# Gate rows and modulation columns of the first turns issued later, and the input of the state scan issued five places sooner in every turn

## What is computed

```
mod = (silu(L0_c) @ L0_wmod).reshape(2, 6, 1, -1)
sa, ca, ga, sb, cb, gb = mod[:, 0], mod[:, 1], ...
ga = (2 * (ga >= 0) - 1) * maximum(abs(ga), 0.25)      # gb the same
h = layernorm(x) * (1 + ca) + sa
x = x + ga * gated_linear_attention(h)                 # chunks of 64, 4 heads
h = layernorm(x) * (1 + cb) + sb
x = x + gb * small_per_channel_mlp(h)
# layer 1, with its own mod from L1_c, L1_wmod
x = x + ga * selective_state_scan(layernorm(x) * (1 + ca) + sa)
x = x + gb * expert_choice_moe(layernorm(x) * (1 + cb) + sb)   # 8 experts
```

## Time and profile before

| what | value |
|---|---|
| median of 3 runs | 1844.66 us |
| the profiled execution | 1847.26 us, span 1845.5 us |
| PE busy | 1696.9 us (92%) |
| DVE busy | 1475.3 us (80%) |
| ACT busy | 1362.8 us (74%) |
| POOL busy | 1369.7 us (74%) |
| first u on DVE | 142.89 us |
| DVE's u of the turns 2 to 15 | every 80.49 us |
| last POOL product of the scan | ends at 1420.8 us |

### The profile page before, as it was taken

How to read it: one execution, slowest core, us unless ns; L and a number is a source line. 1 busy time by engine, 2 the same in 40 slices (tenths; PEclk the granted TensorE clock), 3 DMA queues, 4 the chain that set the end, 5 groups by cost and what they waited for, 6 DMA issues and landing times.

```text
span 1845.5 us, 33565 instructions
## 1 busy us (share of the span) xinstructions
PE 1696.9 (92%) x12092; PEld 1454.0 (79%) x12092; DVE 1475.3 (80%) x3084; ACT 1362.8 (74%) x2673; POOL 1369.7 (74%) x644
## 2 busy tenths in 40 slices
PE   6788999999999999999999999998776999999998
PEld 5566787888878888787888878787565888899997
DVE  3557898898989889888988988888898678766663
ACT  3458879888887988888788888877643756666664
POOL 0008899998989989898998989899999333444443
PEclk8989999999999999999999999999998999999999
DMA  4011121122122112212211221212213444555552
GB/s 195 1 34 65 59 75 66 58 75 82 48 86 75 70 53 75 82 56 82 72 70 61 67 82 61 82 61 80 69 52 99 130 105 108 137 138 137 135 135 29
DMA packets 69461, 149.76 MB, mean 81 GB/s; under 512 B 5936, under 2 KB 43312, under 8 KB 68912
## 3 DMA queue, kind: packets, MB, share of 16 engines
q1 hardware_dynamic: 57008, 130.84, 20.6%
q0 software_dynamic: 12288, 16.79, 5.2%
HBM read 121.91 MB, written 17.30 MB: 75 GB/s over the span
## 4 chain that ended last, share of the span: by engine, by line
PE 73%; DVE 7%; issue 7%; POOL 6%; ACT 6%; DMA 0%; POOLq 0%; DVEq 0%; ACTq 0%
PE po L1820 10%; PE ph L1820 9%; PE pD L1118 9%; PE pY L1135 8%; PE pA L722 6%; DVE room L1167 3%; POOL room L1176 3%; PE pB L914 3%; PE pB L924 3%; POOL room L1186 3%; PE pB L1214 3%; PE pB L945 2%; PE pA L621 2%; PE pA L656 2%; PE pB L930 2%
## 5 line engine op out<-in xcount | busy, mean ns | idle before, releaser
L1186 POOL TENSOR_TENSOR room<-room 128x1024 f32<-128x1024 f32 x256 | 607.2, 2372 | 168.7 <-DVE room L1101 144.0
L1167 DVE TENSOR_TENSOR_SCAN room<-pD,last,room 128x256 f32<-128x256 f32 x1024 | 690.1, 732 | 43.0 <-PE pD L1118 31.7
L1176 POOL TENSOR_TENSOR room<-room 128x1024 f32<-128x1024 f32 x256 | 607.3, 2373 | 62.1 <-PE pY L1135 61.5
L1148 ACT ACTIVATE room<-room,fixed,kkT 128x512 f32<-128x512 f32 x512 | 406.6, 807 | 54.7 <-PE pD L1118 52.7
L1118 PE MATMUL pD<-fixed,room 128*128 128x128 f32 x2048 | 316.6, 278 | 60.3 <-DVE room L1167 49.1
L1135 PE MATMUL pY<-fixed,room 128*128 128x128 f32 x2048 | 315.5, 277 | 11.4 <-POOL room L1176 11.4
L1118 PEld LDWEIGHTS pD<-fixed,room 128*128 128x128 f32 x2048 | 240.0, 143 | 93.2 <-issue 44.1
L1135 PEld LDWEIGHTS pY<-fixed,room 128*128 128x128 f32 x2048 | 246.6, 144 | 61.6 <-POOL room L1176 24.1
L341 POOL DMA_INDIRECT xg<-xn_rows,W x64 | 67.5, 1054 | 196.5 <-DVE W L335 181.0
L1779 ACT ACTIVATE h<-ph 128x512 f32<-128x512 f32 x128 | 76.7, 599 | 137.8 <-PE ph L1820 107.1
L1820 PE MATMUL po<-w_up,h_up 128*128 128x256 f32 x512 | 149.6, 292 | 3.2 <-DVE h_rest L1687 2.6
(11 more groups left out here) (313 smaller groups left out, 3507.4 us busy)
## 6 DMA issues: line engine op xcount, KB each, us to landing
room<-kq_rows SPq DMA_DIRECT2D x128, 512.0 KB, 3.9
w_in<-w_d SPq DMA_DIRECT2D x32, 1024.0 KB
room<-ndS SPq DMA_DIRECT2D x16, 512.0 KB, 3.2
xt<-x_in SPq DMA_DIRECT2D x16, 256.0 KB, 2.9
y_out<-xo SPq DMA_DIRECT2D x16, 256.0 KB, 2.1
xn_rows<-xnC SPq DMA_DIRECT2D x16, 256.0 KB, 2.2
W<-weights SPq DMA_DIRECT2D x1, 1808.0 KB, 9.5
W<-weights SPq DMA_DIRECT2D x1, 1697.5 KB, 17.1
```

The lines of the kernel that those rows point to most:

```text
L1148: act.activation(decT[:, m % 2, t, :], turn2(ndT, it, NT * DI, t * DI, DI), ACT.Identity, bias=ones_s[:, 0:1], scale=turn2(kkT, it, NT * D ...
L1167: dve.tensor_tensor_scan(run, pD[h][:, k2 * TB:(k2 + 1) * TB], run, last[:, bass.ds(later(it) * (DS * DT) + m * DT + k, 1)], ALU.mult, ALU ...
L1176: pool.tensor_tensor(sq[:, m % 2], st[:, m % 4], kqb[:, m % SLOTS, 1, :].unsqueeze(1).broadcast_to([P, DT, TB]), ALU.mult).then_inc(sem("r ...
L1186: pool.tensor_tensor(st[:, m % 4], turn2(u, it, DT * TB).rearrange("p (k t) -> p k t", k=DT), kqb[:, m % SLOTS, 0, :].unsqueeze(1).broadca ...
```

## The change

Two things change place. First, in the prologue: layer 0's columns for the second norm move from step 10 to 22 (their copy from 12 to 24), layer 1's columns from steps 18 and 24 of turn -1 to its steps 60 and 63, the first three gate rows from 12, 18 and 69 to 34, 64 and 73, and the first fold from 34 to 44. The fold is split: `wo_g` needs only the first gate and stays with it, `wout_g` and the bias wait for the second gate and move to step 69. Second, u moves from 69 to 64 in all turns.

```
-    sig1=56, den=57, nd=60, ut=61, u=69, ...
+    sig1=56, den=57, nd=60, ut=61, u=64, ...
...
-                    pe.wait_ge(sem("folded"), 1 + B)
+                    pe.wait_ge(sem("folded"), 2)
...
-        MODS_AT, ROWS_AT, OUT_AT = (18, 24), (12, 18, STEPS + 5, STEPS + 20), STEPS + 30
-        FOLDS_AT = (34, STEPS + 5, STEPS + 6, STEPS + 7, STEPS + 8)
+        MODS_AT, ROWS_AT, OUT_AT = (60, 63), (34, STEPS, STEPS + 9, STEPS + 20), STEPS + 30
+        FOLDS_AT = (44, STEPS + 5, STEPS + 6, STEPS + 7, STEPS + 8)
...
-            if n == 10:                     # early_pe: columns of layer 0, second norm
+            if n == 22:
...
-            if n == 12:                     # early_dve: their copy
+            if n == 24:
...
+                dve.wait_ge(sem("grows"), 3)
+                for b in range(B):
+                    for c in range(DC):
+                        i = dve.tensor_tensor(wo_g[:, b, c, :], wo_n[:, c, :], gmul[:, 0, b * D:(b + 1) * D], ALU.mult)
+                i.then_inc(sem("folded"), 1)
+            if n == FOLDS_AT[1]:
                 dve.wait_ge(sem("grows"), 6)
```

More of the change, by code:

```diff
@@ L65 @@
     xs0=45, xs1=46, inz0=50, sz0=46, dkq_mm=50, dkq=52, inz1=51, sz1=52, kturn=53, kk=53, dt0=53, dt1=55, sig0=54,
-    sig1=56, den=57, nd=60, ut=61, u=69, yz0=19, yz1=19, yt0=21, yT0=20, yt1=22, yT1=22, out=25, x_scan=28, ln_d=40,
+    sig1=56, den=57, nd=60, ut=61, u=64, yz0=19, yz1=19, yt0=21, yT0=20, yt1=22, yT1=22, out=25, x_scan=28, ln_d=40,
     rows_d=42, turn_d=74, mod_d=75, score=79, scores=81, dec=11, sum=22, open0=21, open1=24, dec_t=6, saved=21,
@@ L1375, in early_dve @@
                 dve.wait_ge(sem("folded"), 1)
+                dve.wait_ge(sem("grows"), 3)
[4 more added lines that the diff above has]
+            if n == FOLDS_AT[1]:
                 dve.wait_ge(sem("grows"), 6)
                 for b in range(B):
-                    ga0, gb0 = (gmul[:, g, b * D:(b + 1) * D] for g in range(2))
-                    for c in range(DC):
-                        dve.tensor_tensor(wo_g[:, b, c, :], wo_n[:, c, :], ga0, ALU.mult)
+                    gb0 = gmul[:, 1, b * D:(b + 1) * D]
                     dve.tensor_tensor(wout_g[:, b, :], fo("wout2"), gb0, ALU.mult)
-                    dve.tensor_tensor(bg[:, b, :], fo("bout"), gb0, ALU.mult).then_inc(sem("folded"), 1)
+                    i = dve.tensor_tensor(bg[:, b, :], fo("bout"), gb0, ALU.mult)
+                i.then_inc(sem("folded"), 1)
             for part, at in enumerate(FOLDS_AT[1:4]):
                 if n == at:
-                    dve.wait_ge(sem("folded"), 1 + B + 2 * part)
+                    dve.wait_ge(sem("folded"), 3 + 2 * part)
                     dve.tensor_copy(bpart[:, :, :], bg[:, :, :]).then_inc(sem("folded"), 1)
-                    dve.wait_ge(sem("folded"), 1 + B + 2 * part + 1)
+                    dve.wait_ge(sem("folded"), 3 + 2 * part + 1)
                     row = slice(32 * part, 32 * part + 1)
```

## The result

| kernel | median | lowest to highest | runs | ratio to before, 95% interval |
|---|---|---|---|---|
| before | 1844.36 us | 1842.62 to 1845.01 | 6 | |
| after | 1853.03 us | 1851.28 to 1853.65 | 6 | 1.0047 [1.0036, 1.0058] |

The change makes the kernel 8.7 us slower. The profiled execution of after took 1851.96 us, with a span of 1850.1 and a mean granted clock of 0.975.

What follows compares the result with a forecast made beforehand. PE was taken to pace inner turns, POOL the last ones. Prologue -1.0, first boundary +0.3 and inner turns +11.3 make +10.6 us, 1844.66 to 1855.3 us; forecast range 1851 to 1860.5, 8-in-10 range 1845.5 to 1861.

Steps and rivals of the forecast that it cites:

- Part 1: Turn ends: u ahead of the statistics delays `og` and PE's restart by 0.87 us, 13 times, 11.3 us lost.
- The cushion: DVE's wait for ACT ahead of `og`, 0.31 us, taken off u's length of 1.18 us.
- the first boundary: First turn end with u: DVE waited 0.96 us ahead of `og`, so only 0.3 us is lost.
- Part 2: Prologue up to L630: products moved off the chain gain 6.7 us, 8.1 if z is fast, 5.2 if slow.
- Part 3: Prologue work put back on the chain in three groups, costing 1.8, 2.0 and 1.9 us.
- (a): First gate row ahead of the scores, with DVE operations and fold behind it: costs 1.8 us.
- (b): Two column groups and second gate row around the sum of squares: cost 2.0 us, bounds 0.8 and 4.
- (c): Third gate row moved onto the chain just before L890: costs 1.9 us, bounds 0.4 and 3.2.
- A: Rival: the turns absorb u's delay, only the prologue's effect is left, 1844.0 us; chance 0.11.
- D: Rival: prologue as forecast, but only half of the loop's delay carries, 1849.7 us; chance 0.10.
- B: Rival: POOL gains from the sooner u, 0.28 us in each of thirteen turns, 1840.1 us; chance 0.06.
- C: Rival: all 1.18 us count in 14 turns and the prologue loses its upper bound, 1865.8 us; chance 0.07.

Runs made afterwards that it cites:

- experiment 1: Kernel after, with its changed prologue, but u back at its old step 69: 1843.22 us against 1844.46, ratio 0.9993.
- experiment 2: Kernel before, with its old prologue, and only u moved, to step 64: 1853.84 us, ratio 1.0052.
- experiment 4: Kernel before with u at step 67, behind `og` and ahead of the sum: 1862.3 us, ratio 1.0091.
- experiment 5: Kernel before with u at step 68, which gave DVE the same instruction order as step 67: 1861.96 us, ratio 1.009.
- Experiment 7: Kernel after with u at step 69 and the third gate row back at its old step: 1841.76 us, ratio 0.9981.
- experiment 9: Kernel after with u at 69, third gate row at its old step and layer 1's columns behind the sum of turn 0: 1838.76 us, ratio 0.9965.
- experiment 3: Kernel before, u kept at step 69, its two products computed a second time into scratch at step 64: 1856.8 us, ratio 1.0058.
- experiment 6: Kernel before with u behind the sum and its statistics, directly ahead of the scan pair PE waits for: 1865.17 us, ratio 1.0109.

## Why the prediction was right

**Direction, mechanism and sum were right.** Forecast 1855.3, measured 1853.0. The prologue's part is small (forecast 1.0 gained, experiment 1: 1.2, not told from none) and u is the whole loss (forecast 11.6, experiment 2: 9.4). In the profiles, after loses 2.67 + 6.64 = 9.3 us against before from the sum of turn 1 to that of turn 15.

**Part 1, size per turn.** Forecast 0.87 us, measured 0.71. The cushion was 0.45 us and not the 0.31 of the wait's row. Before, `og` started 0.32 us behind the listed end of the scan pair ahead of it (776.21 + 1.39 = 777.60, to 777.92; the pair's row is below); without a wait it starts 0.09 ahead of that end (781.07 against 779.77 + 1.39 = 781.16). A row's bracket understates what a queue gains when its wait goes. The other 0.04 is the statistics'.

```profile
776.21 1.39 DVE L1167 TENSOR_TENSOR_SCAN room<-pD,last,room 128x256 f32<-128x256 f32 x2
```

**Part 1, how often.** 13 boundaries were counted. Eleven carry 0.70 us each, give or take 0.02, from the sum of turn 3 (1.10 us ahead of before) to that of turn 14 (6.65 behind): 7.75 us. The two from turn 1 to turn 3 together lose 2.67 - 1.10 = 1.57, unevenly (1.74 and -0.17). I did not follow why, and one trace can't tell: from the sum of turn 1 to that of turn 3 experiments 4 and 5, with the same program order, take 159.00 and 156.90 us. At the first boundary, forecast 0.3, the time from the sum of turn 0 to that of turn 1 is 67.68 us in experiment 2 for 67.56 before. The boundary into the turn that POOL paces carries nothing, as said (6.65, then 6.64). The first u was forecast near 135.3 and came at 131.90; POOL's first product waited for its transfer until 135.60, so this gained nothing.

**Part 1, the place.** The prediction had PE's wait behind the scan pair near 2.5 us instead of 1.64. It stays 1.64: both ends of that stretch, L713 and the scan pair, move together. The extra idle time of PE stands one link earlier, at the product that reads the scan pair ahead of `og`, 0.27 to 1.39 us. And POOL's waits for PE's sums did not rise (4.5 us a turn in both, 62.4 in all for 61.5). Its other waits in a turn are 1.5 for a transfer, 0.4 of issue and 0.3 for DVE, where before had 1.2 for a transfer and 0.6 for PE. The prediction also had PE's low-rank product wait for hA; the earlier trace rows shows no wait there, and after has one of 0.28. The sum did not depend on either place, but someone who looked only at the wait named would have called the mechanism refuted. A delay is to be looked for at the first consumer of the delayed engine, not at the largest wait.

**Part 2.** Forecast 6.7 us at L630 with 8.1 if z is fast; measured 8.2, with z at 2.58, most of it fast. In part that is luck, since two misses offset each other: z started 9.1 us sooner (24.11 for 33.17) and not 8.1, mostly since v was 3.08 long and not 3.76, and 0.9 of it was lost again behind z, where the columns took 3.58 us for 3.15. The behaviour of the clock that was weighed there, by which z would be slow too and the gain 5.2, did not occur.

**Part 3.** Measured between landmarks of the two profiles: (a) the first gate row, forecast 1.8. From L630 to the first key-side transposes L604 it took 9.08 before and 8.82 after, to the second ones 17.18 and 17.68: 0.5 us, under the lower bound of 1.1. But the profile of before was slow there: its q and k product L722 took 4.72 us, in after 3.68. In experiments 2 and 5, with the prologue of before and L722 at 3.72 and 3.65, the two stretches are 7.76 and 15.87, 7.75 and 15.86. Against those (a) is 1.1 us at the first L604 and 1.8 at the second, as forecast. (b) the columns and the second row, forecast 2.0. From there to the sum it took 16.32 and 18.71: 2.4, with one group slow in either (L713 before, the second gate row in after, 3.42). Experiment 7 against experiment 2, where both are fast, gives 17.29 - 14.75 = 2.5. (c) the third gate row, forecast 1.9. From the sum to the next L630 it took 19.46 and 21.05: 1.6; experiments 7 and 9 give 2.5 and 1.1. With like against like the three are 5.8 against 5.7.

**What one profile of the prologue is worth.** Experiments 2 to 6 have the prologue of before, so six executions of it are on record. Their sums of turn 0 stand at 73.52, 70.61, 73.31, 72.13, 70.50 and 73.18. The 3 us between them are the clock at two places. L713 took 3.43 to 3.58 us in four executions and 1.97 in the two short ones, and the L722 behind L630 took 4.54 to 4.83 in the same four and 3.72 and 3.65 in the two.

```profile
68.61 1.97 PE L713 MATMUL pA<-wo_g,og 128*128 128x256 f32 x8 [2.29 <-DVE og L871]
```

This is experiment 2's, where the earlier trace rows had 3.53. The profile of before was one of the long ones here, and with 422.4 us one of the long ones behind the scan; both push it above its median, and so its comparison with after towards 4.7 us where the medians show 8.7. Term (b) took 1.5 us back for a fast L713 as if it had always been slow, and in after the slow stretch fell on the gate row ahead of it. What decides it in an execution stays open.

**The rivals.** A (absorbed) and D (half) fall by experiment 2. B falls in the inner turns by experiment 3, and nothing shows it at the end. C (all of u's length in every turn) does not hold at this slot. At another, experiment 6, 1.16 of the 1.18 us reach PE's wait, though the turn loses 0.75 before the clock.

## What to carry to other kernels

- A move in an engine's queue is priced by its slot: the operation's length, less what the next instruction on the critical chain had been waiting. Against its old place behind the scan pair, the same 1.18 us cost 0.3 us a turn ahead of the sum, 0.71 ahead of `og` and 0.75 directly ahead of the pair, before the clock added 1.2 to 1.4 at some of these places. The rule gives how late the chain gets, and the turn can lose less: directly ahead of the pair PE's wait grew by 1.16 and the turn by 0.75. To be ready sooner is worth nothing where the consumer is not the pace.
- The two profiles of before and after put a price of 0.5 us on a gate row that cost 1.8. Where the same product takes 4.72 us in one execution and 3.7 in another, prices come from profiles in which it ran alike.
- A copy of the moved operation at the new place, with the original left alone, separates the cost of the time from the use of the sooner result in a single run.
- A total such as 144 us of waiting for one releaser should be split into its number and its longest before it is taken for a reason to move anything: here it was one wait in the prologue.

## What the runs showed that was not expected

- PE's waits of 1.93 and 2.80 us at a turn's end were often followed by a granted clock of 0.72 to 0.75 over 6 us, which costs 1.2 to 1.4 us of the turn, several times the 0.3 of the wait itself. With 1.64 us, in before, and with 1.39 and 1.64 us some four microseconds apart, in after, the clock stayed at 1.00 in the turns looked at.
- It is not fixed by the wait: experiment 4 had three turns of some twelve at full clock, experiment 5, the same program order, none, and experiment 6 every second one.
